# Attention stage: VectorE makes the low part of projected rows behind the next unit's two maxima instead of in front of them

## What is computed

```
q = split_heads(x @ Wq + bq)
k = split_heads(x @ Wk + bk)
v = split_heads(x @ Wv + bv)
attn = einsum('bhqd,bhkd->bhqk', q, k) / sqrt(HEAD_DIM)
attn = attn + alibi                      # a column vector for each head
attn = where(causal, attn, finfo.min)
p = softmax(attn, axis=-1)
out = einsum('bhqk,bhkd->bhqd', p, v)
return out @ Wo + bo
```

## Time and profile before

| | |
|---|---|
| three runs | 1866.65, 1869.94, 1870.73 us; median 1869.94 us |
| the profiled execution | 1869.54 us |
| its span, first to last instruction | 1867.4 us |
| around the span | 2.1 us |
| mean granted clock of TensorE over the span, as a share of the full one | 0.993 |
| busy share of the span | PE 96%, DVE 71%, ACT 51%, POOL 31% |

### The profile page before, as it was taken

The page is one execution under the profiler, slowest core; times in us unless marked ns, Lnnn a source line. Parts: engine busy times, 40 slices in busy tenths (PEclk is TensorE's granted clock), DMA queues, the critical chain, the costliest instruction groups (busy, mean ns, idle before and its releaser), DMA issues.

```text
span 1867.4 us, 26671 instructions
## 1 busy us (share of the span) xinstructions
PE 1791.4 (96%) x9573; PEld 1382.1 (74%) x9573; DVE 1332.9 (71%) x1870; ACT 950.2 (51%) x1807; POOL 580.6 (31%) x399
## 2 busy tenths in 40 slices
PE   7999999999799999998799999999999998999999
PEld 6888888888354545534578888888888886777888
DVE  6666666567999999999976666565676556777533
ACT  3542323333688768787645433233334327988422
POOL 1000143100388879888730000000000024655000
PEclk9999999999899999999999999999999999999999
DMA  5232335211122222223203233132121306663100
GB/s 200 83 96 74 99 119 164 63 62 35 52 75 71 75 79 74 71 68 117 81 18 81 73 97 104 63 107 63 63 71 56 65 1 125 114 128 74 38 12 23
DMA packets 84203, 146.41 MB, mean 78 GB/s; under 512 B 13864, under 2 KB 23720, under 8 KB 83560
## 3 DMA queue, kind: packets, MB, share of 16 engines
q1 hardware_dynamic: 84072, 144.72, 27.3%
HBM read 130.38 MB, written 14.29 MB: 77 GB/s over the span
## 4 chain that ended last, share of the span: by engine, by line
PE 78%; DVE 11%; issue 5%; ACT 4%; POOL 2%; DMA 0%; DVEq 0%; SPq 0%; POOLq 0%; ACTq 0%
PE psum L161 20%; PE psum L162 19%; PE psum L163 19%; PE psum L1521 6%; DVE scan_state L1722 5%; PE psum L1375 2%; PE psum L2124 2%; POOL scan_state L1249 1%; ACT attn_p L2272 1%; PE psum L1473 1%; PE psum L278 1%; DVE moe_hidden_lo L866 1%; PE psum L2078 1%; DVE X L822 1%; PE psum L2141 1%
## 5 line engine op out<-in xcount | busy, mean ns | idle before, releaser
L793 ACT ACTIVATE moe_hidden_hi<-moe_hidden 128x512 fp32r<-128x512 f32 x200 | 126.3, 631 | 399.2 <-DVE moe_hidden L846 398.3
L1249 POOL TENSOR_TENSOR scan_state<-scan_delta_u,scan_B_rows 128x1024 f32<-128x1024 f32 x127 | 299.3, 2367 | 80.5 <-PE psum L1521 59.5
L161 PE MATMUL psum<-xnT_hi,moe_w_hi 128*128 128x512 f32 x800 | 316.5, 396 | 2.6 <-DVE xnT_lo L475 2.3
L162 PE MATMUL psum<-xnT_lo,moe_w_hi 128*128 128x512 f32 x800 | 314.5, 393 | 0.0
L163 PE MATMUL psum<-xnT_hi,moe_w_lo 128*128 128x512 f32 x800 | 312.4, 390 | 0.0
L1722 DVE TENSOR_TENSOR_SCAN scan_state<-psum,scan_state 128x1024 f32<-128x1024 f32 x128 | 291.4, 2281 | 0.3
L842 DVE TENSOR_TENSOR moe_gated_up<-moe_gate_rows,psum 128x512 f32<-128x512 f32 x184 | 126.6, 688 | 210.1 <-PE psum L163 124.7
L423 POOL TENSOR_SCALAR rstd<-mean_var 128x2 f32<-128x2 f32 x48 | 10.6, 220 | 743.2 <-DVE mean_var L457 743.1
L161 PE MATMUL psum<-moe_w_hi,moe_hidden_hi 128*128 128x256 f32 x800 | 230.3, 288 | 3.6 <-DVE moe_hidden_lo L866 2.2
L1521 PE MATMUL psum<-scan_state,ident 128*128 128x512 f32 x480 | 228.4, 599 | 2.2 <-DVE scan_gated L1737 1.4
L163 PE MATMUL psum<-moe_w_hi,moe_hidden_lo 128*128 128x256 f32 x800 | 226.2, 283 | 0.0
(11 more groups left out here) (234 smaller groups left out, 3503.4 us busy)
## 6 DMA issues: line engine op xcount, KB each, us to landing
scan_B_rows<-scan_B SPq DMA_DIRECT2D x127, 256.0 KB, 3.1
moe_gate_rows<-gate_table SPq DMA_DIRECT2D x176, 128.0 KB, 3.0
moe_w_raw<-moe_pack SPq DMA_DIRECT2D x50, 384.0 KB, 4.1
attn_stack<-attn_rows SPq DMA_DIRECT2D x96, 128.0 KB, 5.8
moe_gate_rows<-gate_table SPq DMA_DIRECT2D x32, 224.0 KB, 3.2
ffn_w_raw<-ffn_pack SPq DMA_DIRECT2D x16, 384.0 KB, 4.4
moe_gate_rows<-gate_table SPq DMA_DIRECT2D x32, 160.0 KB, 2.6
moe_gate_rows<-gate_table SPq DMA_DIRECT2D x24, 192.0 KB, 2.9
```

What stands on the lines that cost most here:

```text
L161: e.matmul(out, wH, xH, start=start, stop=False)
L162: e.matmul(out, wH, xL, start=False, stop=False)
L793: e.activation(self.hH[:, b, :], self.hb[:, b, :], ACT.Copy).then_inc(self.s_hH.sem, 1)
L1249: e.tensor_tensor(self.st[q % self.NBUF][:], self.dtu[:, 2 * h:2 * h + 2, :], self.Bs[:, q % self.RING, :].unsqueeze(1).broadcast_to([P, 2 ...
```

## The change

The low part of a q or k projection made in unit `n` is taken out of the end of unit `n` in VectorE's list and put into unit `n+1`, behind `recip`, `first` and `second` of that unit. Jobs that are not q or k rows stay. Twelve low parts move: `q0`, `k0`, `q1`, `k1` in chunks 0, 1 and 2, from units 1, 2, 4 and 5 into 2, 3, 5 and 6. Those made ahead of the loop stay too.

```
+        def rows_of(n):
+            it = self.job(*divmod(n, self.UNITS), 1)
+            return bool(it) and it[0][0] in "qk"
+
...
                 second(n + 2)
+            if n and rows_of(n - 1):
+                job(*divmod(n - 1, self.UNITS), 1)
             norm(c, u)
             job(c, u, 0)
             keep(n)
             if n and n % 2 == 0:
                 out_lo(n // 2 - 1)
-            job(c, u, 1)
+            if not rows_of(n):
+                job(c, u, 1)
```

## The result

| | before | after |
|---|---|---|
| median of 8 runs each, same chip | 1870.49 us (1866.65 to 1871.74) | 1878.07 us (1874.03 to 1879.35) |
| the profiled execution | 1869.54 us, span 1867.4 | 1878.48 us, span 1876.5 |
| mean granted clock of TensorE over the span | 0.993 | 0.990 |

The ratio is 1.0036, with a 95% interval from 1.0025 to 1.0048: slower, by 4.7 to 9.0 us. The prediction said 1874.8 us, some 5 us more than before; it has the sign and the mechanism, and is too small by about 2.5 us. The measured median lies just above its range (1870.5 to 1877.5); the ratio on the three runs of before that the prediction knew (1869.94) gives 1876.7. The eight executions after lie in two groups, three from 1874.03 to 1874.89 us and five from 1878.06 to 1879.35, and the profiled one is of the second.

What follows compares the result with a forecast made beforehand. PE was taken to set the pace through most of the stage. Job waits 0.6, loads 0 + 1.8 + 1.2 and a clock fall 1.7 made 5.3 us over 1869.54, so 1874.8 us, range 1870.5 to 1877.5.

Steps and rivals of the forecast that it cites:

- The maxima gain nothing: Attention, twelve places: first maxima start at most 0.66 us earlier, entered in the sum with nothing.
- The jobs: PE's next projection job waits about 0.1 us for the low part at six places: +0.6 us.
- The loads: Loads behind k0's low part go 1.79 us later; PE's masks wait: 0, +1.8, +1.2 us for units 8, 16, 24.
- Unit 16: PE's mask for unit 16 waits for the later landing of its last load: +1.8 us.
- Unit 24: Later landing delays unit 24's mask and its first score, to 1677.85 from 1676.63: +1.2 us.
- Unit 8: Mask could start at 1588.06 and starts at 1588.55 now, so the later landing costs 0.
- The clock: TensorE's clock falls behind the new waits for loads; one paid fall taken, +1.7 us, bounds none and three.
- one paid fall: Main case: late loads plus one fall of TensorE's clock that costs 1.7 us, giving 1874.8 us; chance 0.42.
- a fall at two or all three places: Rival at the waits for loads: 7.0 us, 1876.5 us, or 1878.2 with three falls; chance 0.14.
- POOL: Rival on DVE: the low part waits for POOL's multiplication, 12 us, above 1885 us; chance 0.02.
- Quick loads: Rival at the masks: the last load takes 7.4 us throughout, 1.5 us in all, 1871.0 us; chance 0.17.
- the gain: Rival: loads land in time and PE's waits for ACT shrink by about 2.3 us, 1867.2 us; chance 0.05.

Runs made afterwards that it cites:

- e6: The changed kernel with three jobs exchanged in the table, so that k0 and its 12 loads come a unit earlier: 1867.95 us, ratio 0.9989.
- e9: The kernel before with the same three jobs exchanged, so that k0 and its loads come a unit earlier: 1868.10 us, ratio 0.9986.
- e1: The change, but the low part of k0 stays in its old place (9 of 12 move): 1869.35 us, ratio 0.9994 against the kernel before.
- e7: The change with only the low parts of q0 and k1 moved (6 of 12): 1870.84 us, ratio 1.0003 against the kernel before.
- e2: The change with only the low part of k0 moved (3 of 12): 1876.28 us, ratio 1.0028 against the kernel before.
- e5: The kernel before, DVE's order untouched, with SPq held ahead of the writes of k0's rows until the next unit's second maximum: 1876.82 us, ratio 1.0030.
- e3: The changed kernel with SPq loading a half's q rows directly behind their own writes: 1874.84 us, ratio 1.0019 against the kernel before.

## Why the prediction was right, and where it was short

**The maxima gain nothing: right.** They start 0.33 us behind the score, 0.66 earlier, as worked out. At the moved places ACT's waits got shorter, as said (unit 13's from 0.71 to 0.51 us), and five of 28 are gone; their total did not shrink, because those at units 8, 16 and 24, 0.51 us each before, grew with PE's waits for the loads to 1.30, 2.26 and 2.61. What reached PE are waits for ACT of 0.41, 0.29 and 0.27 us, in units 6, 14 and 22 of the kernel before, which are gone. They lie ahead of the masks that wait for loads, and these waits take them back. `e6` against `e9` shows the same by a measurement.

**The jobs: right in size, not seen in the total.** PE starts the job 0.11 us later, where 0.1 was said. Behind it, from unit 12's mask to unit 13's and from unit 20's to 21's, PE takes 5.68 and 5.67 us, before 5.60 both times (1610.19 to 1615.79, 1654.11 to 1659.71). `e1` and `e7`, which move the low part of `q0`, have 5.67 to 5.69 there; `e2` and `e5`, which don't, 5.59 to 5.60. So such a wait is paid with 0.07 to 0.09 us at these two places. Where `v0` waits for `k1`, the after kernel's trace names a wait in unit 6 and none in units 14 and 22, where PE has just waited longer for the loads. And jobs that the sum left out wait too, `k1` for `q1` and `out1` for `k0`: they are five of the nine weight loads. In the time of a whole execution none of it can be told: `e1` is below the kernel before, `e7` 0.2 us above it.

**The loads: right in kind, term by term off by up to 0.9.**
- Unit 16, 1.8 forecast, 1.37 measured. The last load started 8.85 us behind the last early score (1619.45 to 1628.3), before 7.05 (1616.85 to 1623.9): later by the 1.8 as said. But it took 8.0 us and not 8.6.
- Unit 24, 1.2 forecast, 2.1 measured (3.72 less the clock). The last load took 7.3 us, less than before (7.8), but one of the twelve had been held 1552 ns at its issue, where the others take 426: the twelve took SPq 6.71 us instead of 5.60. That is 1.1 later, of which 0.5 came back in the landing.
- Unit 8, 0 forecast, 0.56 measured. The last load took 8.3 us and not 7.4. This is inside the bound of 0.7 that was kept for it.

Unit 24's twelve loads in SPq's timeline, after and then before:

```profile
1670.02 6.71 SPq L1958 DMA_DIRECT2D attn_stack<-attn_rows  x12
```

```profile
1662.65 5.60 SPq L1958 DMA_DIRECT2D attn_stack<-attn_rows  x12
```

From the first issue to the last landing that is 13.6 us for 13.0. In `e2` and `e5` it is 12.4, and there unit 24's term is 0.8 and 1.0 us (45.99 and 46.12 us from unit 16's mask to unit 24's, less 43.56 and the fall). So part of the 2.1 is the luck of this execution.

With the jobs' share they are 4.05 us (7.15 less 3.1 for the clock), where the sum without the clock had 3.6. The landing time was the loosest figure indeed, and it moved to both sides.

**The clock is the term that was too small.** The sum took one paid fall; the profile shows two, behind unit 16's and unit 24's waits, of 1.6 and 1.5 us (1.7 forecast). The rival "a fall at two or all three places", 7.0 us with two, is what this execution shows: 7.15. It had 0.14. Two steps made it so low. First, the prediction set one fall against the seven waits of the earlier trace rows. The trace of the kernel before has three falls in that stretch, the first and the last of them not in the earlier trace rows:

```profile
1547.50:1550.50 3.00, 3.00 (x15) 2.88 (x16) 3.00 (x5) 1.50 (x8) 0.00 (x0) 0.50 0.36 135
1578.00:1581.00 3.00, 3.00 (x18) 2.63 (x20) 2.66 (x7) 2.49 (x13) 2.19 (x3) 0.50 1.10 150
1714.50:1717.50 3.00, 3.00 (x18) 2.53 (x19) 3.00 (x4) 2.60 (x14) 2.67 (x2) 0.50 0.00 0
```

They follow waits for ACT that end at 1546.75, 1576.82 and 1713.26 (1.33, 1.32 and 1.17 us). Two waits of the seven that are nearly as long, 1.32 us at 1557.80 and 1.09 at 1697.88, have no fall behind them, and the other two are of 0.29 and 0.27 us. So among the waits of over 1 us three of five were followed by one. Second, the argument that one fall shortens what PE would wait for next did not hold. The slow stretch behind unit 16 ends at 1640.94, and the loads of unit 24 start 29 us later and are themselves set by PE's scores: from unit 16's mask to the first of them it is 33.60 us (1636.42 to 1670.02), before 30.10 (1632.55 to 1662.65), later by the 1.8 and the fall.

Two is not the number for every execution. `e2` and `e5` show one paid fall each in their profiles, none behind the shorter waits at unit 24 (1.01 and 0.78 us), and these executions are 3.7 and 2.8 us over the median of the kernel before, where the medians are 5.6 and 6.2 over it. Of the other executions only the mean granted clock is on record, not the place of a fall. In `e5` it is 0.992 to 0.994 in the five executions of 1873.0 to 1874.2 us and 0.989 to 0.991 in the six of 1876.8 to 1879.3. One fall of 3.4 us at 0.50 takes 0.001 off the mean, so the longer ones had about three more falls somewhere in the program, as an estimate. How many of them the change brings about stays open.

**The rivals.** POOL did not hold up the low part. The tile `attn_rows_lo` in the after kernel, 14 of them (ns, shortest, median, longest):

```profile
L2225 DVE SCALAR_TENSOR_TENSOR attn_rows_lo<-psum,attn_bq_scaled,attn_rows_hi x7: 742/742/752, 1548.7 to 1678.9; 128x512 fp32r<-128x512 f32 x7
L2225 DVE SCALAR_TENSOR_TENSOR attn_rows_lo<-psum,attn_bk,attn_rows_hi x7: 742/742/744, 1549.4 to 1686.8; 128x512 fp32r<-128x512 f32 x7
```

They take 0.74 us as ahead of the change, though POOL's multiplication now runs beside the low part (1619.94, for 2.90 us, around the row at 1621.50). "Quick loads" and "the gain" fall with the landing times: the last loads of the after kernel took 8.3, 8.0 and 7.3 us, and all three masks waited. By the rate that the Trainium skill gives for transfers into SBUF (SBUF — State Buffer, section "A bandwidth-pool intuition that's wrong (but worth ruling out)"), 436 GB/s, the loads would have been in long before, by the prediction's estimate from it. The trace disagrees again, by the same 7.3 to 8.3 us for the last load alone.

## What to carry to other kernels

Moving an operation behind others on an engine that has time to spare moves everything that its semaphore releases, and the longest chain behind it decides: here 0.74 us of DVE's work stood ahead of a write to DRAM and 12 loads with no slack. So follow each moved instruction to the last transfer that it starts, and if that has no slack, first move the producer up (here its job, by a unit). Where a change adds waits on PE at several places, keep a fall of the clock at each of them within the range: in the profiles here it came behind one or two of the three, and behind waits of 1.1 to 1.3 us elsewhere in the stage sometimes and sometimes not. Count first, over the whole stretch, how often waits of that length have a fall behind them already.

## What the runs showed of the hardware that was not expected

- In `e3` the two writes of a k half that stand right behind six loads in SPq's queue land 5.0 to 5.2 us after their issue (around 1624 us). In the after kernel the same writes, with no loads ahead of them, land in 2.0 to 2.4 us. To split a group of loads so that a part starts earlier can delay the write that the rest waits for.
- One issue on SPq now and then takes 1.2 to 2.1 us instead of 0.43. In the after kernel two of the attention's last seven groups of twelve took 6.71 and 7.38 us, the others 5.47 to 5.58; in the kernel before none. It is no safe sign of a late landing: in `e2` a group that took 7.08 us to issue had its last load in 12.4 us after the first issue, and undisturbed ones took up to 13.7. What holds the issue, and what sets the 12.4 to 13.7 us, stays open.
- At units 8, 16 and 24 the clock fell behind PE's waits for loads of 1.61, 1.79, 2.22 and 2.35 us and not behind those of 0.18 to 1.20 us. But the length of the wait does not decide by itself. At unit 4 the clock did not fall behind 2.24 us in the kernel before and 2.27 in `e2`, and it fell behind 1.63 in `e3`; waits for ACT of 1.17 to 1.33 us had a fall behind them and had none. In the lead-in of the after kernel the clock was 0.50 from 1559.02 to 1565.85, where the kernel before, with the same instructions there, had 1.00. What decides between them the runs don't show.
